# Graph layers and routed experts on one core: how the edge heads reach the partitions, and which engine splits the first x

## The reference, cut to what matters

```python
x = x + gnn(layernorm(x), weights, roots, ..., edge_index=[src, dst], edge_type_4)
x = x + ffn(layernorm(x))

def gnn(X, ...):                      # 4 layers, N = 3125 nodes, 256 features, 4 relations
    cnt = zeros((N, 4)).at[dst, etype].add(1.0)
    inv_deg = 1.0 / maximum(cnt[dst, etype], 1.0)
    for l in range(4):
        h = einsum('ni,rio->rno', X, W[l])
        agg = segment_sum(h[etype, src] * inv_deg[:, None], dst, N)
        out = agg + X @ root[l] + bias[l]
        X = elu(norm(out) * gamma[l] + beta[l]) + X
    return X

def ffn(x):                           # 8 experts, the best 2 for each row
    xn = norm(x) * gamma + beta
    w, idx = softmax(top_k(xn @ Wr + br, 2))
    return sum_e w_e * (gelu(xn @ W1[e] + b1[e]) @ W2[e] + b2[e])
```

## Time and profile before

| | us |
|---|---|
| median of 3 runs | 2293.65 |
| lowest, highest | 2291.12, 2296.48 |
| span of the profiled execution, which is the only time it has | 2581.8 |

### The profile page before, as it was taken

How to read it: one execution, slowest core, us unless ns; L and a number is a source line. 1 busy time by engine, 2 the same in 40 slices (tenths; PEclk the granted TensorE clock), 3 DMA queues, 4 the chain that set the end, 5 groups by cost and what they waited for, 6 DMA issues and landing times. The chain is left out here.

```text
span 2581.8 us, 46238 instructions
## 1 busy us (share of the span) xinstructions
PE 2075.7 (80%) x16327; PEld 1296.1 (50%) x16327; DVE 1572.2 (61%) x4475; ACT 818.3 (32%) x1674; POOL 1253.4 (49%) x1223
## 2 busy tenths in 40 slices
PE   0576788787879889898889888898987988774992
PEld 0334455454545455555545545454554645454992
DVE  5976677575656356566553656566364766575665
ACT  1564556454456011111111212111011111123992
POOL 2124333544430266666716666662665656752441
PEclk9988899988889899899989999999997999986996
DMA  5698333444432487666637867765775655532335
GB/s 144 187 273 256 115 112 115 133 123 125 122 112 98 145 256 233 219 210 210 187 113 249 257 210 240 236 218 158 230 231 165 181 163 169 179 101 64 95 94 178
DMA packets 211755, 445.56 MB, mean 173 GB/s; under 512 B 40819, under 2 KB 137088, under 8 KB 209733
## 3 DMA queue, kind: packets, MB, share of 16 engines
q1 hardware_dynamic: 138357, 274.65, 34.6%
q0 software_dynamic: 61408, 156.79, 20.1%
q10 hardware_dynamic: 11760, 11.08, 1.7%
HBM read 338.14 MB, written 103.90 MB: 171 GB/s over the span
## 5 line engine op out<-in xcount | busy, mean ns | idle before, releaser
L1421 POOL DMA_INDIRECT n_BIG<-n_xd,n_SIDX x1080 | 1110.9, 1029 | 1091.2 <-PE n_PS L1907 501.3
L1888 PE MATMUL n_PS<-n_BIG 125*128 125x500 f16 x4800 | 1196.8, 388 | 69.3 <-issue 45.3
L1888 PEld LDWEIGHTS n_PS<-n_BIG 125*128 125x128 f16 x4800 | 441.1, 100 | 508.7 <-issue 142.0
L1907 PEld LDWEIGHTS n_PS<-n_OW,n_BIG 128*128 128x128 f16 x4320 | 256.3, 99 | 204.6 <-issue 68.9
L1907 PE MATMUL n_PS<-n_OW,n_BIG 128*128 128x84 f16 (+21 forms) x4320 | 303.5, 201 | 51.5 <-issue 41.6
L1927 PE MATMUL n_PS<-n_BIG,n_tabs 128*128 128x256 f16 x2400 | 299.3, 280 | 19.4 <-issue 18.9
L1601 DVE TENSOR_TENSOR n_ST<-n_PS,n_INVB 128x500 f32<-128x500 f32 x200 | 199.9, 1041 | 158.4 <-issue 47.6
L1927 PEld LDWEIGHTS n_PS<-n_BIG,n_tabs 128*128 128x128 f16 x2400 | 239.7, 101 | 62.9 <-issue 29.0
L1627 DVE SCALAR_TENSOR_TENSOR n_U<-n_PS,n_cw,n_BI 125x256 f32<-125x256 f32 x100 | 48.2, 482 | 334.9 <-PE n_PS L1927 161.3
L1296 ACT ACTIVATE n_BIG<-n_PS 128x500 f16<-128x500 f32 x300 | 164.3, 578 | 195.5 <-PE n_PS L1859 93.6
L1312 ACT ACTIVATE n_tabs<-n_ST 128x1000 f16<-128x1000 f32 x100 | 103.8, 1038 | 358.8 <-DVE n_ST L1601 192.3
(11 more groups left out here) (271 smaller groups left out, 2252.9 us busy)
## 6 DMA issues: line engine op xcount, KB each, us to landing
n_BIG<-n_a SPq DMA_DIRECT2D x175, 625.0 KB
n_a<-n_BIG SPq DMA_DIRECT2D x12, 3125.0 KB
n_xg<-n_tabs SPq DMA_DIRECT2D x53, 481.9 KB
n_INVB<-n_ind SPq DMA_DIRECT2D x100, 250.0 KB
n_BIG<-n_xd,n_SIDX POOLq DMA_INDIRECT x1080
n_BIG<-in_L_ffn_W_dram SPq DMA_DIRECT2D x32, 512.0 KB
n_xd<-n_BIG SPq DMA_DIRECT2D x75, 112.0 KB
n_whl<-n_BIG SPq DMA_DIRECT2D x16, 512.0 KB
```

The costliest lines, as they stand in the source:

```text
L1421: e.indirect_dma_start(m.GR[:, g % GS, :], None, m.XD[l % 2][:, :], bass.IndirectOffsetOnAxis(ap=m.SIDX[:, i:i + 1], axis=0)).then_inc(s[f ...
L1888: ins = e.matmul(m.bank(2 * p + h, 0, W), m.xps[l % 2][0:TN, part, D * k + 128 * h:D * k + 128 * h + 128], m.RA[0:TN, c.slot_of(n), W * (k ...
L1907: ins = e.matmul(m.bank(2 * p + h, at, c.width[q]), m.GR[:, g % GS, D * part + 128 * h:D * part + 128 * h + 128], ow, start=(first == 0 an ...
```

## The change

The heads are multiplied by the identity on VectorE (`HM`: 125 partitions x 25 x 125, all zero but the own block of each partition) and summed over the partitions by seven f32 products with a matrix of ones, which leaves them on all partitions in PSUM. The DRAM tensor and its three DMAs go. The compares read PSUM. ScalarE normalizes x in place of VectorE (`Identity` with bias and scale), before the flag. The high halves move from the preparation into ScalarE's part of the build, one ahead of each `os` of VectorE's and each block until the 25 are made. GpSimd makes the low halves with two instructions each at the head of its program. `rsqrt` moves ahead of `scales_near`. `c.order` and `sync_program` stay as they are. In the dense program, which doesn't run with these inputs, some registers are loaded one at a time.

```diff
-        self.HB = raf[:, 5664:5664 + NH]
+        self.HM = raf[0:TN, 5664:5664 + NH]
+        self.ONF = raf[0:TN, 11448:11576]
...
 def prep_sync(e, a, c, m, s):
-    e.wait_ge(s["heads"], 1)
-    for p, n in ROWS:
-        e.dma_start(m.HD.rearrange("(p e) -> p e", p=TN)[p:n], m.HDS[p:n, :]).then_inc(s["hd"], 16)
-    e.wait_ge(s["hd"], 32)
-    e.dma_start(m.HB, m.HD.partition_broadcast(128)).then_inc(s["hd"], 16)
     e.wait_ge(s["keys"], 3)
...
 def prep_scalar(e, a, c, m, s):
-    e.wait_ge(s["scales"], 1)
+    e.wait_ge(s["norm"], 1)
     for t in range(T):
-        e.wait_ge(s["ln"], t + 1)
-        e.activation(m.halves(0, t)[0], m.X[0:TN, t, :], ACT.Copy, scale=m.scale[0:TN, 0:1]).then_inc(s["hi0"], 1)
+        e.activation(m.X[0:TN, t, :], m.X[0:TN, t, :], ACT.Identity, bias=m.nt[0:TN, 0, t:t + 1],
+                     scale=m.nt[0:TN, 3, t:t + 1]).then_inc(s["ln"], 1)
...
 def prep_tensor(e, m, s):
+    e.wait_ge(s["heads"], 1)
+    for at in range(0, NH, 512):
+        n = min(512, NH - at)
+        ins = e.matmul(m.PS[:, at:at + n], m.ONF, m.HM[:, at:at + n], start=True, stop=True)
+    ins.then_inc(s["hd"], 1)
+    e.wait_ge(s["pool_const"], N_CONST)
     e.wait_ge(s["bad"], 1)
-    e.wait_ge(s["pool_const"], N_CONST)
...
 def prep_vector(e, q, a, c, m, s, flag):
     e.wait_ge(s["dst"], 32)
-    e.tensor_copy(m.HDS[:, :], m.DST[:, 0:NE // TN:HEAD]).then_inc(s["heads"], 1)
+    q.did(e.tensor_copy(m.HDS[:, :], m.DST[:, 0:NE // TN:HEAD]))
+    q.did(e.memset(m.ONF, 1.0))
+    q.then()
+    e.wait_ge(s["pool_const"], N_CONST)
+    e.tensor_tensor(m.HM.rearrange("p (k e) -> p k e", k=TN), m.HDS.unsqueeze(1).broadcast_to([TN, TN, NH // TN]),
+                    m.ident[0:TN, 0:TN].unsqueeze(2).broadcast_to([TN, TN, NH // TN]), ALU.mult
+                    ).then_inc(s["heads"], 1)
...
-    e.wait_ge(s["hd"], 48)
+    e.wait_ge(s["hd"], 1)
...
-        q.did(e.tensor_scalar(m.CMP[:, 0:high - low], m.HB[:, low:high], m.tb[:, 0, i:i + 1], 0.0, ALU.is_lt, ALU.add,
+        q.did(e.tensor_scalar(m.CMP[:, 0:high - low], m.PS[:, low:high], m.tb[:, 0, i:i + 1], 0.0, ALU.is_lt, ALU.add,
...
         q.did(e.bn_aggr(m.mv0[0:TN, t, :], m.bs0[0:TN, t, :]))
+    q.then()
+    rsqrt(e, q, m, m.mv0[0:TN, :, 1], m.nt[0:TN, 3, :])
+    q.then()
+    e.scalar_tensor_tensor(m.nt[0:TN, 0, :], m.mv0[0:TN, :, 0], -1.0, m.nt[0:TN, 3, :], ALU.mult, ALU.mult
+                           ).then_inc(s["norm"], 1)
     scales_near(e, q, m, s)
-    rsqrt(e, q, m, m.mv0[0:TN, :, 1], m.nt[0:TN, 3, :])
-    q.then()
...
-    for t in range(T):
-        e.tensor_scalar(m.X[0:TN, t, :], m.X[0:TN, t, :], m.mv0[0:TN, t, 0:1], m.nt[0:TN, 3, t:t + 1],
-                        ALU.subtract, ALU.mult).then_inc(s["ln"], 1)
...
 def scalar_program(e, a, c, m, s):
     e.wait_ge(s["pool_const"], N_CONST)
+    e.wait_ge(s["scales"], 1)
+    e.wait_ge(s["ln"], T)
+    halved = 0
     for what, l, i in c.order:
+        if what in ("os", "block") and halved < T and (what == "block" or c.maker(i) == "v"):
+            e.activation(m.halves(0, halved)[0], m.X[0:TN, halved, :], ACT.Copy, scale=m.scale[0:TN, 0:1]
+                         ).then_inc(s["hi0"], 1)
+            halved += 1
...
 def gpsimd_program(e, a, c, m, s):
+    k = Own(e, s["pool_const"], N_CONST)
+
+    def scaled(t):
+        if t >= 4:
+            e.wait_ge(s["xp"], t - 3)
+        k.did(e.tensor_scalar(m.U[0:TN, t % 4, :], m.X[0:TN, t, :], m.scale[0:TN, 0:1], None, ALU.mult))
+
+    e.wait_ge(s["scales"], 1)
+    e.wait_ge(s["ln"], T)
+    scaled(0)
+    for t in range(T):
+        hi, lo = m.halves(0, t)
+        if t + 1 < T:
+            scaled(t + 1)
+        e.wait_ge(s["pool_const"], N_CONST + t + 1)
+        e.wait_ge(s["hi0"], t + 1)
+        e.tensor_tensor(lo, m.U[0:TN, t % 4, :], hi, ALU.subtract).then_inc(s["xp"], 1)
...
 def vector_program(e, done, a, c, m, s):
-    for t in range(T):
-        hi, lo = m.halves(0, t)
-        e.wait_ge(s["hi0"], t + 1)
-        e.scalar_tensor_tensor(lo, m.X[0:TN, t, :], m.scale[0:TN, 0:1], hi, ALU.mult, ALU.subtract
-                               ).then_inc(s["xp"], 1)
...
 def tensor_program(e, a, c, m, s):
-    e.wait_ge(s["ln"], T)
```

More of the change, by code:

```diff
@@ L57 @@
 PADE = 4096
-PREP = """dst src ety heads hd keys ev table off rows_near rows_far rel bad flag_pe flag x_in consts scales ln
+PREP = """dst src ety heads hd keys ev table off rows_near rows_far rel bad flag_pe flag x_in consts scales norm ln
 hi0 xp xd0 pool_const v_own b1 fc""".split()
@@ L685, in __init__ @@
         self.EV = dram("ev", (2 * (NE + PADE),), F32)
-        self.HD = dram("hd", (NH,), F32)
         self.IND = dram("ind", (T, W), F32)
@@ L1002, in prep_vector @@
         q.did(e.bn_aggr(m.mv0[0:TN, t, :], m.bs0[0:TN, t, :]))
-    scales_near(e, q, m, s)
+    q.then()
     rsqrt(e, q, m, m.mv0[0:TN, :, 1], m.nt[0:TN, 3, :])
     q.then()
+    e.scalar_tensor_tensor(m.nt[0:TN, 0, :], m.mv0[0:TN, :, 0], -1.0, m.nt[0:TN, 3, :], ALU.mult, ALU.mult
+                           ).then_inc(s["norm"], 1)
+    scales_near(e, q, m, s)
     e.wait_ge(s["rows_near"], 16 * c.PT)
@@ L1066, in scales_near @@
     e.sem_inc(s["scales"], 1)
-PREP_DONE = dict(dst=32, src=32, ety=32, heads=1, hd=48, keys=3, ev=48, table=16, off=1, rel=1, bad=1, x_in=32,
-                 consts=32, b1=16, fc=32, scales=1, ln=T, hi0=T, pool_const=N_CONST)
+PREP_DONE = dict(dst=32, src=32, ety=32, heads=1, hd=1, keys=3, ev=48, table=16, off=1, rel=1, bad=1, x_in=32,
+                 consts=32, b1=16, fc=32, scales=1, norm=1, ln=T, pool_const=N_CONST)
 def prep_over(e, c, s):
@@ L2657, in dense_scalar @@
     e.wait_ge(s["prep"], c.prep["gp_sub"])
-    regs = [e.alloc_register(f"er{TD}_{i}") for i in range(BATCH)]
     for t in range(TD):
@@ L2664, in dense_scalar @@
         for i in range(GPT):
[L2665 to L2668, removed]
+            at = GPT * t + i
+            e.wait_ge(s["slot_free"], e.value_load(m.egrow[0:1, at:at + 1], min_val=1, max_val=c.P) + S8)
             e.activation(rows[:, :, 20 * i:20 * i + 20], m.bank((GPT * t + i) % 4, 0, W).rearrange(
@@ L3092, in dense_tensor @@
     e.wait_ge(s["prep"], c.prep["b1t"])
-    regs = [e.alloc_register(f"pr{TD}_{i}") for i in range(3 * BATCH)]
+    regs = [e.alloc_register(f"pr{TD}_{i}") for i in range(2 * BATCH)]
     n_os = 0
@@ L3096, in dense_tensor @@
         n = min(BATCH, c.P - p0)
-        for w in range(3):
+        for w in range(2):
             at = w * c.PT * 128 + p0
@@ L3107, in dense_tensor @@
                 e.wait_ge(s["os"], n_os) if n_os else None
-                last = 2 * BATCH + min(i + 1, n - 1)
-                e.wait_ge(s["evac"], e.snap(regs[last], min_val=1, max_val=c.G + 1))
+                last = 2 * c.PT * 128 + p0 + min(i + 1, n - 1)
+                e.wait_ge(s["evac"], e.value_load(m.tabrow[0:1, last:last + 1], min_val=1, max_val=c.G + 1))
             e.matmul(m.PS[:, bass.ds(clear, 2)], m.OS[:, p % S8, :], m.Z[:, :], start=True, stop=False,
```

## The result

The changed kernel takes **2309.36 us** in the median of four runs (2306.8 to 2313.05) against 2292.39 for the kernel before (four runs, 2288.69 to 2296.48): ratio 1.0079, 95% interval 1.0058 to 1.01, some 17 us slower. The execution profiled here, 2306.8 us by its own time, has on the page's first line

The account below looks back on a forecast made before the run. SP's in-order queue, started by the last low half, was taken as what ends last. PE's 19.8 us gain is spent waiting; X 16.3 later less closed holes gives +3.6 us, 2297.3 us, range 2283 to 2311.

Parts of the forecast that it names:

- The forecast (SP's start eats the gain): SP's queue starts later with the last low half, using up PE's 19.8 us earlier start: +3.6 us, chance 0.55.
- rival B: Build: GpSimd and VectorE get in each other's way, 12 us later, sum +15.6, 2309 us; chance 0.18.
- Heads: Preparation: heads by products are there at 19.8 instead of 29.72 us, offsets 9.6 us earlier.
- Edges' store: Preparation: store issued at 16.0; if landed by 30, gathered rows come before VectorE asks; +5 us kept otherwise.
- rival C: Preparation doesn't deliver: edges' store lands at 37, flag and X 5 later, +8.6, 2302 us; chance 0.07.
- Normalizing: Preparation: normalizing leaves VectorE, 8.16 us fewer before the flag; flag at 48.0, first pair at 57.7 instead of 77.48.
- X, the last low half: Build: the last low half, on GpSimd, comes at 93 instead of 76.67, 16.3 later, bounds 87 and 105.
- From X to the counts: SP's queue: both holes (10.25 and 2.50 us) close, 62.96 us left; counts at 155.96 against 152.38, +3.6.
- VectorE in front of the maximum: Build: VectorE reaches `wmax` at about 111 and waits for the weights; the maximum ends 123.1 to 135.2.
- Behind the counts: After tile 0's counts: the wait at 217 moves along and all engines follow the same list; no further change.
- a first degree after 168: PE's first degree, expected near 162: after 168 would mean the forecast is wrong, pointing to rival B.
- Rival A: Queue isn't the bound outside the profile, stores and fills at 0.7 of their time: -7.2, 2286.5 us; chance 0.20.

Follow-up runs that it names:

- e10: The changed kernel itself again, on the chip of the experiments: 2606.06 us against 2588.39 for the kernel before, ratio 1.0074.
- e11: The changed kernel with its 54 zero fills issued in the idle time of SP's queue: 2555.96 us, ratio 0.9898 to the kernel before.
- e9: Kernel before with product heads, ScalarE normalizing, both halves in the preparation and 54 fills in the queue's idle time: 2547.18 us against 2588.39, ratio 0.986.
- e4: Kernel before, with GpSimd also doing fifty operations beside the build into a buffer nobody reads: 2630.51 us, ratio 1.0058.
- e5: Changed kernel with the low halves on VectorE inside the build, two places behind their high halves: 2623.57 us against 2610.81 for the kernel before, ratio 1.0056.
- e12: Kernel before with its 54 zero fills issued in the idle time of SP's queue: 2558.51 us against 2589.26, ratio 0.9872.
- the first attempt: Three kernels, the one before and the changed one among them, with fills six behind each of layer 0's first nine new-x stores: ratios 1.004, 1.0055, 1.0088.
- e7: Changed kernel with all 54 fills issued later, six behind each of the first nine stores of layer 0's new x: 2624.1 us, ratio 1.0055.

## Why the prediction was right and where it was off

The forecast (SP's start eats the gain) named the mechanism that the runs show, and its range held the result. It put the size at +3.6 us where +17 was measured, so the centre was 12 us too low, and the time came out at the price that rival B had (2309). The forecast's own span, -2.4 to +8.6 us, doesn't reach +17: the range held the result only because it had been drawn out past B's price, and that is luck. "Slower" had been given the largest chance (0.45), though only 0.20 of it by the forecast's own way. By its steps:

- *Heads.* 19.8 forecast, 18.23 measured. `HM` took 3.42 (3.9), the products 7.73 (8.5, bounds 5.6 and 11.3), reading PSUM nothing (0.3). The Trainium skill (FP8 and Floating Point Precision, TensorE Precision Notes) with its four passes gave by my estimate 5.2 at one clock level and 10.4 at the other. The trace lies between them and agrees with both in turn: of the fourteen weight loads for seven products the early ones are 0.86 us apart and, from 14.86 us on, the others 0.43.
- *Edges' store.* The gathers began at 30.45, and VectorE waited 1.34 us for their rows: rival C was not there.
- *Normalizing.* 12.40 us against 11.75, flag 48.20 against 48.0, first pair 55.42 against 57.7.
- *X, the last low half.* 97.78 against 93. The step's 33 us from first pair to last high half went by ScalarE's load; that half ended at 93.78 instead of 90.7, 38.4 us behind the first pair, which is the upper bound of 38.5. But what set X was GpSimd at 1.8 us a tile without a pause, 4.0 us behind that half (2.3 forecast). The upper price in the text, 0.80 us for each of its fifty instructions, was nearly right for the subtractions (0.812) and too low for the scalings (0.995); its 40 us behind a first pair at 57.7 would have given X at 97.7. The bound of 105 isn't worked out in the text. It was dismissed for 0.93 ns an element of a memset, a row of another operation with nothing running beside it. That is the first mis-sized term, **+4.8 us**.
- *From X to the counts.* 69.61 us against 62.96. Both holes closed as forecast (`far_sub` was ready near 102 and not near 96, still ahead of SP). But the six DMAs of the weights took 7.78 us to issue (122.14 to 129.92) against 3.02 (110.90 to 113.92), and `wput` 1.70 against 0.34: +4.76 and +1.36. Before, these issues stood behind holes of 10.25 and 2.50 us. In the first the DMA engines ran empty (share 0.00 from 106 to 111 us); in the second they didn't (1.06 from 126 to 129), and yet `wput` was quick behind it. Taking a hole out of a full queue does not take out the whole hole. That is the second mis-sized term, **+6.65 us**. 3.6 + 4.8 + 6.65 = 15.05, and the counts came 15.0 later. That is from the trace on the fast chip; in e10's it is 72.87 us from X and 18.7 later, so the size of this term is known to some 3 us.
- *VectorE in front of the maximum.* Forecast from 111 until the maximum ends at 123 to 135; it stood from 117 to 137.58. The place was right. VectorE came there 6 us later than forecast because its `hot`s were longer, which cost nothing, as it waited 20.5 us; the weights' issue was 5 us later than forecast (117.0).
- *Behind the counts.* Taken as unchanged. In e10's trace the last tile is issued 23.9 us later than in that of before and the first 18.7; the remaining 5 us weren't followed up, and may lie between chips.

The prediction had named a first degree after 168 as the sign that its forecast was wrong and B right. It came at 174.78, and the `hot`s were longer; by its own mark the forecast had failed and B was right. Only the 20.5 us that VectorE waited in front of the maximum, and e11, show that B's cause is not the one.

*Rival A* (the queue isn't the bound outside of the profile) had the stores and fills at 0.7 of their time; in the trace from the fast chip they took 12.74 and 11.53 us, against 12.37 and 11.56, and e9 shows what the queue is worth. *Rival B* (GpSimd and VectorE in each other's way) has a real contention in it, and a price near what e4 shows (12 forecast, 12.7 measured); but e5, which has none, is nearly as slow, and e11, which has it in full, has its counts earlier than e12. Its time came out for other reasons. The Trainium skill (GPSIMD Engine Reference, Key points) warns of the shared SBUF interface, and the trace agrees that VectorE gets slower: `hot`s, with one tensor input, from 259 to 407 ns, and of the two-input products one group from 670 to 719 ns, while the other (`n_FG`) stayed at 669. My estimate from its two-input figure, 0.56 us for a subtraction, is under the 0.812 measured beside a busy VectorE, and under the shortest, 0.66.

## What to carry to other kernels

Follow the queue that ends last, not the engine: work moved out of the preparation into a loop is delayed by the loop's pace, and if one in-order queue waits for the last piece, all behind it starts that much later. Before moving work, look at what stands in that queue without being needed soon; here 54 fills put into its idle stretches gave the kernel before 1.3%, more than any way of sharing out the work gave (0.5%). A transfer moved out of the way must not land in front of the next urgent one, which is how the first attempt lost all that it had won.

## What the runs showed of the hardware

- GpSimd beside a full VectorE: its scaling of 125x256 f32 took 0.995 us (0.92 ahead of VectorE's first `hot`) and its subtraction 0.812 (0.66 to 1.08). VectorE's `hot`s of 200 columns became 1.57 times as long in the changed kernel and 1.25 times in e4 (259 to 325 ns), where the products of 500 columns became 1.34 times as long (670 to 901). So which instructions pay isn't the same in the two.
- The granted clock column of the kernel before reads 1.00 in its build and that of the changed kernel 0.50 (1.2 GHz of 2.4) in the same work, yet the pair of 200 columns takes 363 and 357 ns. Where the changed kernel's column turns to 1.00, from 107 to 117 us, it takes 248. The products of the heads ran under a column of 1.00 and changed from 0.86 to 0.43 us between two weight loads on the way. So the column at the head of a trace isn't evidence by itself; durations are.
- Issuing a DMA is not of fixed cost: the same six took 3.02 us behind a hole and 7.78 in a queue without one, with the DMA share at 1.03. In e7, right behind the stores of x but with no fills, they took 5.22.
- The same kernel took 2292 us on one chip and 2588 to 2613 on others; the changed one kept its ratio on both (1.0079, 1.0074). The two chips agree at first: the changed kernel issues x at 97.78 and 98.20, tile 0's counts at 167.39 and 171.07. From there to the last tile one takes 588 us and the other 687, with instructions of nearly the same length (VectorE's `hot` of 500 columns 351 and 353 ns, ScalarE's blocks 577 on both); the difference lies between them. Why isn't known.
